# The up product of the node stage by Strassen's scheme: seven block products in place of eight

## What is computed

```python
h = jnp.maximum(_layernorm(x, axis=-1), 0.0)
x = x + segment_sum((h @ W.T)[dst] * edge_weight[:, None], src, N)      # layer 0
h = jnp.maximum(_layernorm(x, axis=-1), 0.0)
h = segment_sum(h[src], dst, N) + h                                     # layer 1
h1 = h @ W1 + b1                                                        # 256 -> 1024
h1 = relu((h1 - mean) * rsqrt(var + 1e-5) * gamma + beta)               # batch norm over nodes
x = x + relu(h1 @ W2 + b2)                                              # 1024 -> 256
```

## Time and profile before

| | us |
|---|---|
| median of 3 runs | 3873.82 |
| lowest and highest | 3873.27, 3875.31 |
| profiled execution | 3883.61 |
| its span, first to last instruction | 3881.8 |
| PE busy | 3433.2 (88%) |
| DVE, ACT, GpSimd busy | 2267.4, 2162.8, 1033.6 |

### The profile page before, as it was taken

The page is one execution under the profiler, slowest core; times in us unless marked ns, Lnnn a source line. Parts: engine busy times, 40 slices in busy tenths (PEclk is TensorE's granted clock), DMA queues, the critical chain, the costliest instruction groups (busy, mean ns, idle before and its releaser), DMA issues.

```text
span 3881.8 us, 56824 instructions
## 1 busy us (share of the span) xinstructions
PE 3433.2 (88%) x17113; PEld 2909.6 (75%) x17113; DVE 2267.4 (58%) x5129; ACT 2162.8 (56%) x3533; POOL 1033.6 (27%) x801
## 2 busy tenths in 40 slices
PE   0378887488877779999999999999999999999999
PEld 0368877477766657778888888888888888888888
DVE  0366665376565668855555555555555655555555
ACT  0255554232222279956666666666666666666665
POOL 6667777688888710000000000000000000000000
PEclk9888888698888889999999999999999999999999
DMA  9988786577777799934333334333333343343342
GB/s 337 335 204 191 191 196 134 121 175 164 161 158 156 160 314 359 360 128 128 111 113 130 108 114 129 108 116 127 108 121 122 108 125 118 110 126 115 112 125 69
DMA packets 305854, 619.82 MB, mean 160 GB/s; under 512 B 34997, under 2 KB 186800, under 8 KB 299856
## 3 DMA queue, kind: packets, MB, share of 16 engines
q1 hardware_dynamic: 229440, 515.46, 39.9%
q0 software_dynamic: 75264, 102.81, 15.5%
q10 hardware_dynamic: 1072, 0.76, 0.1%
HBM read 412.83 MB, written 257.28 MB: 173 GB/s over the span
## 4 chain that ended last, share of the span: by engine, by line
PE 58%; POOL 18%; issue 11%; ACT 6%; another core or an unknown queue 3%; DMA 2%; DVE 1%; ACTq 0%; POOLq 0%; DVEq 0%
PE ps_a L1286 28%; PE ps_b L1300 19%; PE ps_b L1301 9%; POOL x_table L552 7%; POOL agg_table L552 7%; ACT late L685 4%; POOL edge_tiles L542 4%; DMA x_table<-edge_tiles,scatter_now 2%; POOL edge_ring L542 1%; ACT late_r L703 1%; DMA agg_table<-edge_tiles,scatter_now 1%; ACT edge_tiles L631 0%; PE ps_b L1204 0%; DVE edge_same L847 0%
## 5 line engine op out<-in xcount | busy, mean ns | idle before, releaser
L1300 PE MATMUL ps_b<-w_hl,late_r 128*128 128x512 f32 x3128 | 1129.0, 396 | 0.0
L749 ACT ACTIVATE hid<-ps_a,bn_bias,bn_scale 128x512 f32<-128x512 f32 (+1 forms) x784 | 609.1, 777 | 734.9 <-PE ps_a L1286 734.9
L1129 DVE TENSOR_TENSOR late_r<-hid,late_r 128x512 fp32r<-128x512 f32 (+1 forms) x784 | 537.3, 685 | 815.0 <-ACT late_r L754 815.0
L1286 PE MATMUL ps_a<-late_r,w_hi 128*128 128x512 f32 x3136 | 984.0, 395 | 0.0
L1301 PE MATMUL ps_b<-w_hl,late_r 128*128 128x256 f32 x3128 | 876.3, 280 | 0.0
L1300 PEld LDWEIGHTS ps_b<-w_hl,late_r 128*128 128x128 f32 x3128 | 587.6, 188 | 138.9 <-issue 0.5
L1286 PEld LDWEIGHTS ps_a<-late_r,w_hi 128*128 128x128 f32 x3136 | 540.5, 188 | 108.9
L1286 PE MATMUL ps_a<-late_r,w_lo 128*128 128x512 f32 x1568 | 611.8, 390 | 0.0
L1301 PEld LDWEIGHTS ps_b<-w_hl,late_r 128*128 128x128 f32 x3128 | 590.0, 189 | 26.4
L754 ACT ACTIVATE late_r<-hid 128x512 fp32r<-128x512 f32 (+1 forms) x784 | 494.8, 631 | 71.7
L1215 PE MATMUL ps_b<-edge_tiles,edge_same 128*128 128x256 f32 x1568 | 404.2, 423 | 0.0
(11 more groups left out here) (122 smaller groups left out, 4391.3 us busy)
## 6 DMA issues: line engine op xcount, KB each, us to landing
x_rows<-x_table SPq DMA_DIRECT2D x291, 512.0 KB, 4.4
late<-agg_table SPq DMA_DIRECT2D x194, 512.0 KB, 5.7
x_table<-in_x SPq DMA_DIRECT2D x10, 5000.0 KB
agg_table<-zeros SPq DMA_DIRECT2D x40, 1250.0 KB
hT_table<-h_turned SPq DMA_DIRECT2D x388, 128.0 KB, 2.5
hT_f<-hT_table SPq DMA_DIRECT2D x97, 512.0 KB, 3.6
out<-zeros SPq DMA_DIRECT2D x97, 512.0 KB, 6.8
x_table<-edge_tiles,scatter_now POOLq DMA_INDIRECT x196
```

Source lines behind the costliest of these rows:

```text
L749: act.activation(hid[m % 2][:, 0:w].rearrange("p (r a b) -> p r a b", a=BANDS, b=SQUARE), by_row, ACT.Relu, scale=bn_scale[:, m:m + 1], bi ...
L1129: dve.tensor_tensor(hid_lo[m % 4][:, 0:w], hid[m % 2][:, 0:w], hid_hi[m % 4][:, 0:w].bitcast(F32), ALU.subtract).then_inc(hid_lo_ready, 1)
L1286: ins = pe.matmul(ps_a[:, 2 + m % 2, 0:w], w_part[:, kb, cols], h_part[:, kb * w:(kb + 1) * w], start=(t == 0), stop=(t == len(terms) - 1))
L1300: pe.matmul(ps_b[:, r, :], hid_hi[m % 4][:, cols], w2, start=(m == 0), stop=(m == MB - 1), skip_group_check=True)
```

## The change

The product W1 (256 by 1024) times h transposed (256 by 512) is cut anew. Two groups m form a pair i (four pairs per chunk). Of a pair, the weights are a 2x2 matrix of 128x128 blocks A11 to A22, and hT_f is a 2x2 matrix of blocks of 128 by 256, B11 to B22. Strassen's scheme (in Winograd's form, with S1 to S4 sums of A and T1 to T4 sums of B) gives the four results by seven products, called 1 to 7, of three matmuls of 256 columns each. A pair has two PSUM banks in four quarters.

- **PE**: 84 matmuls of 256 columns per chunk for 48 of 512. P1 goes to quarter 0, P5 to 1. Products 6 and 2, then 7 and 3, then 4 are accumulated onto what other engines have put in the quarters. A string per pair (`ORDER`) interleaves them with single down pieces (`d`). Pieces 5 to 7 of m of a chunk run in the next chunk's first two pairs.
- **ACT** copies P1 to quarter 2 and P5 to SBUF (`take_p1_p5`), runs relu on two quarters, and rounds hT_f without B12 (768) and the four T (1024).
- **DVE** adds P5 twice per pair (`add_p5_to_u2`, `add_p5_to_u3`). The sum of h and the norm copies leave it.
- **GpSimd**, idle in this stage before, takes `add_agg` and `pick_norm`, and makes T1 to T4 by four subtractions (`mix_h`).
- **SP**: the nodes of a chunk now lie in PSUM by bands, so a chunk is stored by four DMAs with rows of 1 KB, and x1 for the residual is loaded a second time in that layout (`x1_out`), four more. Buffers shrink: two for x1 and the messages, one each for relu_ln, h, h_turned, hT_f and the table in HBM.
- Once, in the layer-1 edge stage, W1 is mixed and split into seven blocks (DVE, 4 + 7 + 7 operations of 512 elements, for one cast and one subtraction of 2048).

Core of the diff:

```diff
+            def load_x1_out(n, s):
+                for rows, parts, bands in band_rows(x1_table, n):
+                    sp.dma_start(x1_out[s % 2][parts, bands, :], rows).then_inc(x1_out_loaded[s % 2], 16)
...
+            def store(n, s, k):
                 sp.wait_ge(out_ready, n + 1)
-                if load:
-                    load_main(n + LOADS, s)
-                sp.dma_start(chunk_of(out, n), tile_of(out_sb[s % 2], n)).then_inc(out_stored[s % 2], 16)
-                sp.wait_ge(out_stored[s % 2], 16 * turn_of(s, k) + 16)
+                for rows, parts, bands in band_rows(out, n):
+                    sp.dma_start(rows, out_sb[s % 2][parts, bands, :]).then_inc(out_stored[s % 2], 16)
+                if has(n, 2):
+                    load_x1_out(n + 2, s)
+                if has(n, 5):
+                    sp.wait_ge(h_ready, n + 4)
+                    load_main(n + 5, s + 5)
+                if has(n, 3):
+                    turn_h(n + 3)
+                sp.wait_ge(out_stored[s % 2], 16 * ROWS * turn_of(s, k) + moved_rows(n))
                 sp.sem_inc(out_retired, 1)
-            for n in range(LOADS):
...
+            def add_agg(n, s, k):
+                p, j = shape_of(n)
+                pool.wait_ge(ln_ready, n + 1)
+                pool.wait_ge(main_loaded[s % 2], 32 * turn_of(s, k) + 32)
+                if not is_first(n):
+                    pool.wait_ge(turned_ready, n)
+                by_square = h[0].rearrange("p j d -> p (j d)").rearrange("p (c j e) -> p j c e", c=CB, e=SQUARE)
+                pool.tensor_tensor(by_square[0:p, 0:j, :, :],
+                                   relu_ln[0][0:p, 0:j, :].rearrange("p j (c e) -> p j c e", e=SQUARE),
+                                   agg_in[s % 2][0:p, 0:j, :].rearrange("p j (c e) -> p j c e", e=SQUARE), ALU.add).then_inc(h_ready, 1)
+            def mix_h(n):
+                half = width(n) // 2
+                b12, b11, b22, b21 = (hT_f[:, q * half:(q + 1) * half] for q in range(4))
+                t1, t2, t3, t4 = (t_f[:, q * half:(q + 1) * half] for q in range(4))
+                pool.wait_ge(hT_loaded, 16 * n + 16)
+                if not is_first(n):
+                    pool.wait_ge(hT_lo_ready, 2 * n)
+                pool.tensor_tensor(t1, b12, b11, ALU.subtract).then_inc(t1_ready, 1)
+                pool.tensor_tensor(t3, b22, b12, ALU.subtract)
+                pool.wait_ge(t1_ready, n + 1)
+                pool.tensor_tensor(t2, b22, t1, ALU.subtract).then_inc(t2_ready, 1)
+                pool.wait_ge(t2_ready, n + 1)
+                pool.tensor_tensor(t4, b21, t2, ALU.subtract).then_inc(t_ready, 1)
...
+            def relu_hidden(n, m):
+                w = width(n)
+                i, lower = m // 2, m % 2
+                act.wait_ge(up_done, MB * n + m + 1)
+                if not lower:
+                    act.wait_ge(u3_read, PAIRS * n + i + 1)
+                if m >= 2 or not is_first(n):
+                    act.wait_ge(hid_lo_ready, MB * n + m - 1)
+                from_ps = quarters(i)[:, 1:3, 0:w // 2] if lower else quarters(i)[:, 0:4:3, 0:w // 2]
+                act.activation(hid[m % 2][:, 0:w].rearrange("p (v x) -> p v x", v=2), from_ps, ACT.Relu,
+                               scale=bn_scale[:, m:m + 1], bias=bn_bias[:, m:m + 1]).then_inc(hid_ready, 1)
+                if m >= 4 or not is_first(n):
+                    act.wait_ge(down_done, MB * n + m - 3)
+                act.wait_ge(hid_ready, MB * n + m + 1)
+                act.activation(hid_hi[m % 4][:, 0:w], hid[m % 2][:, 0:w], ACT.Copy).then_inc(hid_hi_ready, 1)
+            def take_p1_p5(n, i):
+                half = width(n) // 2
+                act.wait_ge(p1_done, PAIRS * n + i + 1)
+                act.activation(quarters(i)[:, 2, 0:half], quarters(i)[:, 0, 0:half], ACT.Copy)
+                act.activation(p5_sb[:, 0:half], quarters(i)[:, 1, 0:half], ACT.Copy).then_inc(p1_p5_taken, 1)
...
+                for i in range(PAIRS):
+                    take_p1_p5(n, i)
+                    if i == 3 and has(n, 1):
+                        take_mixed(n + 1, s + 1)
+                    if i > 0:
+                        relu_hidden(n, 2 * i - 1)
+                    elif not is_first(n):
+                        relu_hidden(n - 1, MB - 1)
+                    if i < 2 and has(n, 2):
+                        prepare(*after_next(n, s, k), i)
+                    if i == 2 and has(n, 1):
+                        take_hT(n + 1, s + 1)
+                    relu_hidden(n, 2 * i)
...
+                    w1_block = w1_f.rearrange("p k (g h n) -> p k h g n", g=PAIRS, h=2)
+                    a11, a21, a12, a22 = (w1_block[:, kb, half, :, :] for kb in range(KB) for half in range(2))
+                    s1, s2, s3, s4 = (w1_mixed[:, f, :, :] for f in range(4))
+                    chain.then(dve.tensor_tensor(s1, a21, a22, ALU.add))
+                    chain.then(dve.tensor_tensor(s3, a11, a21, ALU.subtract))
+                    chain.wait()
+                    chain.then(dve.tensor_tensor(s2, s1, a11, ALU.subtract))
+                    chain.wait()
+                    chain.then(dve.tensor_tensor(s4, a12, s2, ALU.subtract))
+                    chain.wait()
+                    parts = ((A11, a11), (A12, a12), (A22, a22), (S1, s1), (S2, s2), (S3, s3), (S4, s4))
+                    for at, part in parts:
+                        chain.then(dve.tensor_copy(w1_hi[:, at, :, :], part))
+                    chain.wait()
+                    for at, part in parts:
+                        ins = dve.tensor_tensor(w1_lo[:, at, :, :], part, w1_hi[:, at, :, :].bitcast(F32), ALU.subtract)
+                    ins.then_inc(w12_split, 1)
...
+            def add_p5_to_u2(n, i):
+                half = width(n) // 2
+                dve.wait_ge(p1_p5_taken, PAIRS * n + i + 1)
+                dve.wait_ge(p6_done, PAIRS * n + i + 1)
+                dve.tensor_tensor(quarters(i)[:, 3, 0:half], quarters(i)[:, 2, 0:half], p5_sb[:, 0:half], ALU.add).then_inc(u2_read, 1)
+            def add_p5_to_u3(n, i):
+                half = width(n) // 2
+                dve.wait_ge(up_done, MB * n + 2 * i + 1)
+                dve.tensor_tensor(quarters(i)[:, 1, 0:half], quarters(i)[:, 2, 0:half], p5_sb[:, 0:half], ALU.add).then_inc(u3_read, 1)
...
+                for i in range(PAIRS):
+                    before = not (is_first(n) and i == 0)
+                    last = (n, 2 * i) if i else (n - 1, MB)
+                    if i == 0 and has(n, 1):
+                        turn_squares(n + 1)
+                    if i == 1 and not is_first(n):
+                        read_down(n - 1, s - 1, 0)
+                    if i == 2 and not is_first(n):
+                        finish(*preceding(n, s, k))
+                    if i == 3 and has(n, 1):
+                        hT_low(n + 1, s + 1, False)
+                    if before:
+                        hidden_low(last[0], last[1] - 2)
+                    add_p5_to_u2(n, i)
+                    if i == 1 and not is_first(n):
+                        read_down(n - 1, s - 1, 1)
+                    if i == 3 and has(n, 1):
+                        hT_low(n + 1, s + 1, True)
+                    if before:
+                        hidden_low(last[0], last[1] - 1)
+                    add_p5_to_u3(n, i)
...
+            def product(n, s, i, number):
+                weight, part, to, first = {1: (A11, B11, 0, True), 2: (A12, B21, 0, False), 3: (S4, B22, 3, False),
+                                           4: (A22, T4, 2, False), 5: (S1, T1, 1, True), 6: (S2, T2, 2, False),
+                                           7: (S3, T3, 2, False)}[number]
+                half = width(n) // 2
+                cols = slice(part * half, (part + 1) * half)
+                terms = ((w1_hi, hT_hi), (w1_hi, hT_lo), (w1_lo, hT_hi))
+                for t, (w_part, h_part) in enumerate(terms):
+                    ins = pe.matmul(quarters(i)[:, to, 0:half], w_part[:, weight, i, :], h_part[s % 2][:, cols],
+                                    start=(first and t == 0), stop=(t == len(terms) - 1), skip_group_check=True)
+                return ins
+            def p5(n, s, i):
+                if i == 0:
+                    pe.wait_ge(hT_lo_ready, 2 * n + 2)
+                if i >= 2 or not is_first(n):
+                    pe.wait_ge(hid_ready, MB * n + 2 * i - 2)
+                product(n, s, i, 5)
+            def p1(n, s, i):
+                product(n, s, i, 1).then_inc(p1_done, 1)
+            def p6_p2(n, s, i):
+                pe.wait_ge(p1_p5_taken, PAIRS * n + i + 1)
+                product(n, s, i, 6).then_inc(p6_done, 1)
+                product(n, s, i, 2)
+            def p7_p3(n, s, i):
+                pe.wait_ge(u2_read, PAIRS * n + i + 1)
+                product(n, s, i, 7)
+                product(n, s, i, 3).then_inc(up_done, 1)
+            def p4(n, s, i):
+                pe.wait_ge(hid_ready, MB * n + 2 * i + 1)
```

(2 more changed lines are left out.)

391 lines of the change are left out of this document (219 added, 172 removed).

## The result

The changed kernel is slower: 3921.47 us median (3920.89 to 3923.66) against 3874.57 us for the kernel before on the same chip (3873.27 to 3878.03), a ratio of 1.012 with a 95% interval of 1.0108 to 1.0132. The forecast was 3820 us, in a range from 3778 to 3912. The profiled execution took 3923.66 us, its span 3921.9.

What follows compares the result with a forecast made beforehand. TensorE's matmul stream in the node stage was taken as the bound. Products -101, stalls +39 and one-time costs +8 us took the profiled 3883.6 to 3829.6, against the median 3820; range 3778 to 3912 us.

Steps and rivals of the forecast that it cites:

- Part 1: TensorE products: 84 matmuls at 0.120 us make the chunk's floor 21.28 us, 1.04 less, 101 us over 97 chunks.
- Rival D: TensorE: matmuls of 256 columns cost 0.140 us because of their weight loads, kernel at 3944 us; chance 0.05.
- Part 2: ScalarE load per chunk: eight new PSUM copies add 2.3 us, sum 17.3 of 21.28 us, no bound.
- Rival C: ScalarE's copies from PSUM to PSUM take 0.6 us instead of 0.38, 1.0 us more per chunk, 3878 us; chance 0.12.
- Part 3: VectorE load per chunk rises from 12.8 to roughly 15.6 us of 21.28, not a bound.
- Part 4: New waits of the sixth and seventh products on ScalarE and VectorE: stalls of about 0.1 us per chunk by the rows.
- the walk: Stepping through a pair's instructions by the rows' durations: slack 0.4 and 0.15 us, third pair 0.1 us short.
- The 0.4: TensorE stalls in us per chunk taken for the sum, from 0.1 up to 1.0 possible; 97 chunks make +39 us.
- Part 5: GpSimd's sum of h and four subtractions: 2 to 6 us of 21 per chunk, load hidden; slowing of VectorE left out.
- rival A: VectorE and GpSimd block each other, hidden_low(3) 1.6 us late, 1.3 us lost per chunk, 3907 us; chance 0.25.
- Part 6: Storing and reloading h through memory takes 7.5 us with 5 us spare per chunk; costed at nothing.
- Part 7: One-time costs: tail chunk, final stores, chain before the first chunk, splitting W1; +8 us, bounds 0 to 16.

Runs made afterwards that it cites:

- e10: Kernel before plus one unused GpSimd addition of 1024 elements per chunk, 2.4 us of reading SBUF; 3886.36 us, ratio 0.9999 to the kernel before.
- e13: Changed kernel with GpSimd's sum of h replaced by write-only fills and its four subtractions cut to 8 columns; 3843.11 us, ratio 0.9891 to the kernel before.
- e14: Changed kernel with the sum of h later, u3 before hidden_low in the second pair, the fourth product earlier in the third; 3846.97 us, ratio 0.9917.
- e1: Changed kernel with GpSimd's sum of h started about 1.7 us later by one more wait; 3867.64 us, ratio 0.9953 to the kernel before.
- e3: Changed kernel with GpSimd's sum of h replaced from the third chunk on by two write-only fills; 3866.07 us, ratio 0.995 to the kernel before.
- e8: Changed kernel with ScalarE copying P1 and P5 ahead of the hidden block's high part; 4012.76 us, ratio 1.033 to the kernel before.
- e12: Changed kernel with the sum of h and the subtractions later, and u3 added before hidden_low in the second pair; 3898.68 us, ratio 1.0033.

## Why the prediction was wrong

**What bounds the kernel** was right: PE's stream is the kernel before, and e10 shows how much the other engines could be disturbed without a change.

**Part 1, the products**, was right: 0.120 us per matmul of 256 columns, a product 0.36, a floor of 21.28. Rival D is out.

**Part 2, the copies**, was right: 0.37 us each, 0.30 apart at 2413.52 and 2413.82. Rival C is out. ACT's busy time per chunk is 375.02 x 22.65 / 500 = 17.0 us, 17.3 were worked out.

**Part 3, VectorE.** 380.65 x 22.65 / 500 = 17.2 us per chunk for the 15.6 worked out. The difference is the hold: in that stretch eight hidden_low are 0.2 us longer each than in the earlier trace rows, 1.6 us.

**Part 4, the round trip.** The way was the right one, u3, relu, high part, copies, sixth product, and so was the place of least slack: the walk had the third pair 0.1 us short, and e13 shows it 0.08 late, 0.12 in the whole chunk. But the loss is 0.47 us per chunk without GpSimd's reading in e13, for the walk's 0.1. Three of e13's stalls carry some 0.10 us of restart, which the walk had at nothing: where a slack is just used up, a wait costs 0.1 us more than it lasts. The 0.4 that I took for everything open is nearly the 0.47 of e13. It was written as the price of all the open costs, GpSimd's too, and was used up without GpSimd.

**Part 5, GpSimd, is the step that failed.** Its durations lay in the bounds (2.40 us for the sum, 0.74 for a free subtraction), and the text named the rule, the instruction and the mechanism in rival A; but in the sum of the forecast the hold of VectorE stood at next to nothing, because the one row of before showed GpSimd held by VectorE and not the reverse. It cost 0.90 us per chunk, 87 us over 97. An effect that is shown in one direction between two engines that share something is a reason to expect the other; the prediction gave it to rival A and put nothing for it into the sum. The argument against A, that VectorE is free a quarter of the time and the sum may fall there, was an average. The order of instructions and the timeline gave the place: the sum starts when the relus and norm picks end, and hidden_low(3) is next. That could have been walked as part 4 was.

**Part 6, the way of h**, was right: the load still lands 3.6 us after its issue and PE never waits at a fifth product. **Part 7**: 8 us were taken. The spans differ by 40 us and the chunks account for 33, which leaves 7; by the medians it is 47 - 33 = 14, and in nine of the eleven variants of the changed kernel the same count gives 11 to 16. Either lies within the bounds of 0 to 16; where these us are lost stays open.

**The rivals.** A is what happened, in mechanism and in size: 1.3 us per chunk and 3907 us were given, 1.37 and 3921 measured, 0.4% apart. That is closer than its working deserved, so the nearness of the number is in part luck. As written its terms, 0.85, four times 0.2 and 0.24, add up to 1.9 and not to 1.3; the runs show 0.20 for the four subtractions together, with which they would. It took 1.6 us of lateness for hidden_low(3), where 1.31 was seen, had no restarts, and put down to GpSimd all of what is in part the round trip's own. Its chance of 0.25 was too low, and the range, which left out its worse half, ended 9 us short.

In the sum: forecast -101 + 39 + 8 = -54 against the profiled execution; measured -100 for the products (97 x 1.03), +133 for the stalls (87 by GpSimd's reading, 46 by the round trip), +7 once, together +40. Between the medians it is +47, with 14 once.

What was not tried: the sum and the subtractions split into shorter GpSimd instructions, so that a hold ends sooner, and ScalarE for the subtractions. Whether the last 0.54 us above the floor in e14 can be had is open.

## What to carry to other kernels

When work moves to GpSimd, list VectorE's instructions with two inputs in SBUF, find from the order which of them the new work will meet, and ask who stands behind that one; the load of either engine says nothing. Where a change tightens a round trip between engines, price a wait at its lateness plus a restart of TensorE (0.1 us here), and look for a second round trip over the same engines before moving work from one to the other. And for an operation with freedom to move, as the sum of h or the fourth product, the right place can be worth as much as its removal: e1, which moves the sum, and e3, which leaves it out, have the same ratio.

## What the runs showed of the hardware

- The hold is complete. hidden_low, with two SBUF inputs, ended 0.54 to 0.56 us after GpSimd's reading instruction wherever the two met in 600 us of the changed kernel, e8, e10 and e12 (2411.68 after 2411.13, e10: 2427.42 after 2426.87, e8: 2435.08 after 2434.53), whether it had started 0.6 or 1.8 us into it. As an estimate from these rows, only 0.69 - 0.55 = 0.14 us of its 0.69 are done while it is held.
- It works both ways. A GpSimd subtraction of 256 elements takes 0.74 us; in the changed kernel the third took 1.19 beside a hidden_low and the fourth 1.61 beside finish. So GpSimd's printed time is not the measure of its own work.
- It takes two SBUF inputs. Additions with one input in PSUM kept their 0.43 and 0.69 us beside GpSimd's reading (e1, 2420.22), and fills by GpSimd, which only write, held nothing (e3).
- TensorE, after standing for a semaphore, lost about 0.1 us more: the first two matmuls and the third are 0.34 us apart for 0.24 in the changed kernel; in the variants' timelines at full clock it is 0.07 to 0.11 us.
- TensorE's granted clock fell from 1.00 to 0.50 (1.2 GHz) in e8 behind 9 of the 37 idle times of 1.7 to 1.9 us; in the changed kernel, whose longest idle time at a sixth product is 0.3 us, it stayed at 1.00 through the same stretches.
